# Level 1's loop on the parity form of the composite convolution, with folds one pair ahead and elementwise steps on GpSimd

## The reference: what is computed

```python
for i, typ in enumerate(('same', 'upsample', 'same', 'downsample')):
    s = style @ mod_w[i].T + mod_b[i]
    weight = SCALE * w[i] * s[:, None, :, None]
    weight = weight * rsqrt(sum(weight * weight) + EPS)
    out = conv(out, weight) + biases[i]      # with blur around types 2 and 4
```

```python
W = scales[:, 0][None, :] * q - zeros[:, 0][None, :]
out = einsum('bsi,io->bso', x, W) + bias
```

## Time and profile before

| | |
|---|---|
| median of 3 runs | 907.77 us (907.46 to 908.02) |
| profiled execution, its own time | 907.6 us |
| its span in the trace | 906.1 us |
| PE busy | 898.8 us, 99% of the span |
| DVE busy | 531.7 us, 59% |
| ACT busy | 459.8 us, 51% |
| POOL busy | 89.6 us, 10% |
| store of a pair by POOL, issue to landing (15 of them) | 3.0 us, median |
| granted TensorE clock | 1.000, the upper level (2.4 GHz), all through |

### The profile page before, as it was taken

How to read it: one execution, slowest core, us unless ns; L and a number is a source line. 1 busy time by engine, 2 the same in 40 slices (tenths; PEclk the granted TensorE clock), 3 DMA queues, 4 the chain that set the end, 5 groups by cost and what they waited for, 6 DMA issues and landing times.

```text
span 906.1 us, 15387 instructions
## 1 busy us (share of the span) xinstructions
PE 898.8 (99%) x5174; PEld 825.7 (91%) x5174; DVE 531.7 (59%) x1248; ACT 459.8 (51%) x881; POOL 89.6 (10%) x113
## 2 busy tenths in 40 slices
PE   9999999999999999999999999999999999999998
PEld 8889899899899899899899898888999999999998
DVE  8886445455455455365465465576755566665555
ACT  5955435435445455355355245477455656555540
POOL 0000000000000000000000020302111211111221
PEclk9999999999999999999999999999999999999999
DMA  8701101201201101101102112341222221222111
GB/s 293 247 3 69 69 23 46 69 23 46 69 16 53 50 25 64 46 23 69 46 23 69 62 53 70 65 167 44 93 84 81 93 69 69 69 93 83 57 71 70
DMA packets 33133, 64.30 MB, mean 71 GB/s; under 512 B 11728, under 2 KB 14032, under 8 KB 33104
## 3 DMA queue, kind: packets, MB, share of 16 engines
q1 hardware_dynamic: 24032, 30.90, 11.2%
q0 software_dynamic: 9072, 33.03, 9.7%
HBM read 47.14 MB, written 16.78 MB: 71 GB/s over the span
## 4 chain that ended last, share of the span: by engine, by line
PE 96%; DVE 2%; ACT 2%; issue 0%; ACTq 0%; DVEq 0%
PE conv_ps L184 8%; PE conv_ps L185 8%; PE conv_ps L186 8%; PE fold_ps L728 6%; PE prod_ps L1024 6%; PE prod_ps L1022 6%; PE prod_ps L1023 6%; PE prod_ps L989 5%; PE prod_ps L991 5%; PE prod_ps L990 5%; PE prod_ps L1098 4%; PE prod_ps L1097 4%; PE fold_ps L693 4%; PE turn_ps L943 3%; PE turn_ps L991 2%; PE turn_ps L990 2%
## 5 line engine op out<-in xcount | busy, mean ns | idle before, releaser
L1022 PE MATMUL prod_ps<-b_hi,xt 128*128 128x512 f32 x240 | 93.6, 390 | 0.0
L1024 PE MATMUL prod_ps<-b_hi,xt 128*128 128x512 f32 x240 | 93.5, 390 | 0.0
L1023 PE MATMUL prod_ps<-b_lo,xt 128*128 128x512 f32 x240 | 93.5, 389 | 0.0
L949 ACT ACTIVATE xt<-turn_ps 128x512 fp32r<-128x512 f32 x32 | 17.4, 594 | 136.9 <-PE turn_ps L943 136.9
L989 PE MATMUL prod_ps<-a_hi,xt 128*128 128x384 f32 x240 | 81.2, 338 | 0.0
L991 PE MATMUL prod_ps<-a_hi,xt 128*128 128x384 f32 x240 | 81.1, 338 | 0.0
L990 PE MATMUL prod_ps<-a_lo,xt 128*128 128x384 f32 x240 | 81.1, 338 | 0.0
L1097 PE MATMUL prod_ps<-quant,xt_hi 128*128 128x342 f32 x256 | 80.8, 320 | 0.0
L1098 PE MATMUL prod_ps<-quant,xt_lo 128*128 128x342 f32 x256 | 80.7, 320 | 0.0
L184 PE MATMUL conv_ps<-h_hi,e_hi 128*128 128x512 f32 (+1 forms) x204 | 75.5, 370 | 1.1 <-DVE h_lo L170 1.1
L1082 DVE SCALAR_TENSOR_TENSOR res<-prod_ps,norm,res 128x512 f32<-128x512 f32 x32 | 23.9, 751 | 87.8 <-PE prod_ps L1024 86.7
(11 more groups left out here) (313 smaller groups left out, 2404.0 us busy)
## 6 DMA issues: line engine op xcount, KB each, us to landing
x_in<-in_x SPq DMA_DIRECT2D x64, 128.0 KB, 2.7
res<-in_x POOLq DMA_DIRECT2D x16, 512.0 KB, 3.6
x_after_first<-res POOLq DMA_DIRECT2D x16, 512.0 KB, 2.9
x_in<-x_after_first SPq DMA_DIRECT2D x64, 128.0 KB, 2.7
res<-x_after_first POOLq DMA_DIRECT2D x16, 512.0 KB, 3.5
out_x<-res POOLq DMA_DIRECT2D x15, 512.0 KB, 3.0
a_raw<-in_adapter_in SPq DMA_DIRECT2D x8, 544.0 KB, 8.7
b_raw<-in_adapter_out SPq DMA_DIRECT2D x8, 512.0 KB, 6.9
```

What stands on the lines that cost most here:

```text
L1022: nc.tensor.matmul(prod_ps[n][:, :], bufs.xt_hi[:, k, :], bufs.b_hi[:, k, cols], start=(k == 0), stop=False)
L1023: nc.tensor.matmul(prod_ps[n][:, :], bufs.xt_hi[:, k, :], bufs.b_lo[:, k, cols], start=False, stop=False)
L1024: last = nc.tensor.matmul(prod_ps[n][:, :], bufs.xt_lo[:, k, :], bufs.b_hi[:, k, cols], start=False, stop=(k == KT - 1))
```

## The change

Four things, all in level 1's loop (the last is in code around it):

1. `pe_cond` becomes `pe_three`, with level 0's helpers for the data (`act_layer1_parity`, `act_parity_hi`, `dve_parity_lo`) and filters (`act_fold2_whole`, `act_filters`, `dve_filters`), and with `act_middle` and `dve_join` in the place of `act_cond`.
2. The folds run one pair ahead: step `i` applies the filters of `c` and makes those of `c + 1`.
3. The differences and the sums of filter tiles are made by POOL (`pool_differences`, `pool_filter_sums`), behind `load_residual` and ahead of the next `add_bias`.
4. `pe_turn` comes first in PE's step, and `dve_second_residual` is cut in two: parts 0 and 1 ahead of the split of `x`, part 2 between the two joins.

```diff
+        def pool_differences(pool, c, a, bufs):
+            data = bufs.data[a]
+            odd = data[:, ODD:ODD + SPAN]
+            pool.wait_ge(S.data_pads, DATA_PADS)
+            pool.wait_ge(S.layer1_scaled, 2 * c + a + 1)
+            nc.gpsimd.tensor_tensor(data[:, LEFT:LEFT + SPAN], data[:, EVEN:EVEN + SPAN], odd, ALU.subtract)
+            nc.gpsimd.tensor_tensor(data[:, RIGHT:RIGHT + SPAN], data[:, EVEN + 1:EVEN + 1 + SPAN], odd, ALU.subtract).then_inc(S.differences, 1)
+
+        def pool_filter_sums(pool, c, bufs):
+            pool.wait_ge(S.fold2_hi, 2 * c + 1)
...
+            nc.gpsimd.tensor_tensor(flat(whole[:, E_PAIRS:E_PAIRS + 2, :, :]), flat(whole[:, 0:E_PAIRS:2, :, :]), flat(whole[:, 1:E_PAIRS:2, :, :]),
+                                    ALU.add).then_inc(S.fold2_lo, 1)
...
+                c = f + 1 + AHEAD
+                for a in range(2):
+                    pool_differences(pool, c, a, buf1[slot])
+                if not isinstance(n, int) or j + 1 < SLOTS:
+                    pool_filter_sums(pool, c + 1, buf1[slot])
...
                 c = i + AHEAD
-                pe_layer1(pe, c, 0, bufs)
                 pe.wait_ge(S.x1_ready, evicted(i))
                 pe_turn(pe, i, bufs, True)
-                pe_layer1(pe, c, 1, bufs)
-                pe_fold3(pe, c, bufs)
-                pe_quant(pe, i, 0, bufs)
-                pe_fold2(pe, c, bufs)
-                pe_quant(pe, i, 1, bufs)
+                for a in range(2):
+                    pe_layer1(pe, c, a, bufs)
+                if left:
+                    pe.wait_ge(S.middle_scaled, 2 * c)
+                    pe_fold3(pe, c + 1, bufs)
+                for n in range(2):
+                    pe_quant(pe, i, n, bufs)
+                if left:
+                    pe_fold2(pe, c + 1, bufs)
                 pe_quant(pe, i, 2, bufs)
-                pe_cond(pe, c, 0, bufs)
+                pe_three(pe, c, 0, bufs, left > 0)
...
-                pe_cond(pe, c, 1, bufs)
+                pe_three(pe, c, 1, bufs, left > 0)
...
                 act_turn(act, i, bufs)
-                act_layer1(act, c, 0, bufs)
-                act_fold3(act, c, bufs)
-                act_layer1(act, c, 1, bufs)
-                act_fold2(act, c, bufs)
-                if not last:
+                act_filters(act, c, bufs)
+                act_layer1_parity(act, c, 0, bufs)
+                if left:
+                    act_fold3(act, c + 1, bufs)
+                act_layer1_parity(act, c, 1, bufs)
+                for a in range(2):
+                    act_parity_hi(act, c, a, bufs)
+                if left:
                     split(c + 1, bufs)
-                    act_fold_start(act, c + 1, bufs)
+                    act_fold2_whole(act, c + 1, bufs)
+                if left > 1:
+                    act_fold_start(act, c + 2, bufs)
+                act_middle(act, c, 0, bufs)
...
+                act_middle(act, c, 1, bufs)
                 for a in range(2):
-                    act_cond(act, c, a, bufs)
+                    act.wait_ge(S.cond_out, 2 * c + a + 1)
                     act_ends(act, c, a, bufs)
```

More of the change, by code:

```diff
@@ L867, in act_fold2_whole @@
             nc.scalar.activation(flat(whole[0:C, 0:E_PAIRS, :, C:P]), blocks[C:P, :, :], ACT.Identity)
[L868 to L869 removed]
+            last = nc.scalar.activation(flat(whole[C:P, 0:E_PAIRS - 1, :, C:P]), blocks[0:C, 2:2 * E_PAIRS, :], ACT.Identity)
+            if not bufs.first_sample:
+                last = nc.scalar.activation(whole[C:P, E_PAIRS - 1, :, C:P], bufs.e_hi[C:P, E_PAIRS - 1, :, C:P].bitcast(F32), ACT.Identity)
+            last.then_inc(S.fold2_hi, 1)
         def dve_filter_sums(v, c, bufs):
@@ L891, in dve_filters, with pe_three @@
             low(flat(bufs.sum_lo[:, :, :, :]), flat(bufs.whole[:, E_PAIRS:E_PAIRS + 2, :, :]), flat(bufs.sum_hi[:, :, :, :])).then_inc(S.fold2_ready, 1)
-        def pe_three(pe, c, a, bufs):
+        def pe_three(pe, c, a, bufs, ahead=False):
+            if a == 1 and ahead:
+                pe.wait_ge(S.fold2_hi, 2 * c + 3)
             if a == 0:
@@ L1120, in dve_second_residual @@
                     nc.vector.tensor_tensor(bufs.res[:, cols], bufs.res[:, cols], bufs.scaled[:, cols], ALU.add).then_inc(S.y_ready, 1)
-            if not last:
+            if not last and 2 in parts:
                 v.wait_ge(S.zeros_added, g + 1)
@@ L1189, in program @@
             b.xt_hi, b.xt_lo = T1(f"xt_hi1{n}", [P, KT, P], F32R), T1(f"xt_lo1{n}", [P, KT, P], F32R)
+        data1, whole1 = [T1(f"data1{a}", [P, DATA]) for a in range(2)], T1("whole1", [P, E_PAIRS + 2, 2, P])
+        for b in buf1:
+            b.data, b.whole = data1, whole1
+            b.sum_hi, b.sum_lo, b.right_hi, b.right_lo = buf0.sum_hi, buf0.sum_lo, buf0.right_hi, buf0.right_lo
         level1.close()
@@ L1355, in _, with second_step @@
             add_bias(FIRST % SLOTS, 1)
-            with pool.Fori(0, (END - FIRST - 1 - AHEAD) // SLOTS) as n:
-                for j in range(SLOTS):
[L1358 to L1363, removed]
+            def second_step(n, j):
+                f = SLOTS * n + (FIRST + j)
+                slot = (FIRST + j) % SLOTS
+                add_bias((slot + 1) % SLOTS, n + (1 if j + 1 < SLOTS else 2))
+                store_output(f, slot)
+                pool.wait_ge(S.y_stored, 16 * (f - NPAIR) + 16)
+                load_residual(f + SLOTS, slot)
+                c = f + 1 + AHEAD
[3 more added lines that the diff above has]
+                    pool_filter_sums(pool, c + 1, buf1[slot])
+            loops = (END - FIRST - 1 - AHEAD) // SLOTS
+            with pool.Fori(0, loops - 1) as n:
+                for j in range(SLOTS):
+                    second_step(n, j)
+            for j in range(SLOTS):
+                second_step(loops - 1, j)
             for f in range(END - 1 - AHEAD, END - 1):
@@ L1915, in _ @@
             dve_first_residual(v, f, buf0)
+            nc.vector.memset(whole1[C:P, E_PAIRS - 1, :, C:P], 0.0)
+            for a in range(2):
+                dve_data_pads(v, c, a, slot(c))
             edge_copies(v, set1, buf0)
```

89 lines of the change are left out of this document (56 added, 33 removed).

## The result

The changed kernel takes 917.19 us (median of 4 runs, 915.38 to 918.14); the kernel before took 907.88 beside it (907.46 to 908.02). The ratio is 1.010, interval 1.008 to 1.012: slower by 1.0%. The profiled execution took 916.77 us, with a span of 915.2, against 907.6 and 906.1 before. The granted clock is 1.000 in both of these executions, so nothing of their difference is the clock's.

The account below looks back on a forecast made before the run. PE was taken to bound the old kernel, a 17.7 us ring grown to 20.75 by collisions the new one. Twelve steps 244.35, + 3.6 at the start, - 238.0 before = +9.95 on 907.6: 917.5 us, range 903 to 922.

Parts of the forecast that it names:

- PE's saving, 1.22 us a pair: Level 1's convolutions on PE in parity form: 4.35 us a pair instead of 5.57, making a step 18.5 us.
- Start, +3.6: Ahead of the loop: +2.9 us for the fold that comes in on PE, +0.7 for the wait for the third `scaled`.
- The two collisions, +0.95 and +2.1: Split of `x` on VectorE: first half waits 0.95 us for GpSimd's sum of filters, second half 2.1 for `add_bias`.
- rival B: Sum of filters starts a little after VectorE's split of `x` instead of 0.15 before: 904 to 911 us, chance 0.20.
- the slack: Room of 0.8 us between the walk without collisions, 17.7, and PE's 18.5; the first step still has it.
- Rival C: Engines hardly hinder one another, so PE bounds eleven steps of 18.5 us: 895, range 892 to 898, chance 0.15.
- The differences: GpSimd's two differences of a=1, 257 columns: 0.74 us each, 1.6 for two with signals.
- The line: Cost estimate for GpSimd operations between measured sizes: 2.18 ns a column over 0.18 us.
- the ring: From a step's last join through ACT, POOL, ACT and DVE back to it: 17.7 us, 20.75 with collisions.
- the nine: The steps between the second and the last of level 1's loop: 20.75 us each, 186.75 together.
- The last step: Twelfth step, without fold: 16.5 us of PE work, plus waits of 0.8 for transposed data and 1.5 for `scaled`: 18.8.
- The one that waits gets the next turn: Between GpSimd and VectorE, a two-input SBUF operation waits for the other's whole operation, then goes next; shown waits 0.21, 0.45 us.

Follow-up runs that it names:

- experiment 4: Changed kernel with the loop's add_bias cut from 1024 columns to one, its place and semaphores kept: 896.55 us.
- Experiments 1 to 5: Changed kernel with differences and filter sums on VectorE 897.51 us; sums alone there 905.54; differences alone 911.52; add_bias cut to one column 896.55; in two halves 908.32.
- experiment 7: Changed kernel with add_bias moved from behind the sum of filters to ahead of the differences, directly behind load_residual: 919.29 us.
- experiment 6: Changed kernel with add_bias replaced at its place by a one-input GpSimd operation (res times 1.0, 128x1024): 902.84 us.
- experiment 1: Changed kernel with differences and sums of filters on VectorE, add_bias staying on GpSimd: 897.51 us.
- experiment 8: Kernel of experiment 7 with load_residual, the DMA issue ahead of add_bias, moved behind the sum of filters: 900.84 us.
- experiment 5: Changed kernel with add_bias as two GpSimd operations of 512 columns at its place: 908.32 us.
- experiment 9: Kernel of experiment 7 with a GpSimd wait between load_residual's DMA issue and add_bias, until sum_lo is done: 907.42 us.

## Why the prediction came out

- **PE's saving, 1.22 us a pair: right.** 4.32 us for a pair, first step 18.58 for 18.5, and 18.5 in every step of experiment 4.
- **Start, +3.6: right.** Between the first two sets of transposes lie 14.98 us; before it was 640.80 - 628.11 = 12.69, with a first convolution of 1.4 in it that now stands behind them. 14.98 - 11.3 = 3.7, of which 0.70 is the wait for `scaled` that was named.
- **The two collisions, +0.95 and +2.1: right**, to 0.1, and so were their order and the margin of it (`x_lo` comes up 0.14 behind the start of the sum; I had 0.15). It held in ten of the eleven steps that have a sum. In the first one the order was rival B's: the two `x_lo` begin at 656.34, the sum only at 656.67, the first `x_lo` goes free and the second takes 1.79; there the slack covered it, and PE did not wait for the transposes behind. Experiments 1 to 5 show that these collisions make the loss. Rival C is what the kernel is with nothing in the way: 895 foreseen, 896.55 and 897.51 measured.
- **The differences: mis-sized.** The line gave 0.74 us for 257 columns; they took 0.64. That takes 0.2 off the ring: second step 20.07 for 20.3, the nine 20.56 for 20.75. In all 1.9 us too much.
- **The last step: a wait missed.** From 866.58 to the first product behind it (887.07) are 20.49 us, where I had 18.8, so 1.7 too little. That step has no sum of filters, so `add_bias` follows the differences at once and meets `_lo` of a=0. At that place I had counted only a collision with a difference, and put it at nothing because VectorE waits there for ScalarE; `add_bias` I had left out of this step:

```profile
877.05 2.61 DVE L170 TENSOR_TENSOR right_lo<-data,right_hi 128x257 fp32r<-128x257 f32 x1
```

  PE stood 1.4 us for it. The two mistakes cancel: 244.2 us for the twelve steps, 244.35 foreseen. Where the trace ends within 0.7 us of the forecast, some of that is luck. The sum with these measured terms is still 0.8 above the 9.1 us between the two spans, and that lies in the kernel before: its steps are 19.80 us on average (640.80 to 858.59 is eleven of them), where the one that I read had 19.76, so its twelve steps take 238.55 us (from the first convolution at 639.39 to the first product behind them at 877.94), not 238.0; and it reaches its first transposes 0.23 later (628.11, now 627.88).
- **"The one that waits gets the next turn": right here, wrong as a rule.** It holds where the waiting one comes up during the other's operation, as all through the changed kernel, and fails behind a DMA issue (experiment 7). Had the change left `add_bias` there, the same working would have given 897 for a kernel of 919, and would have missed the falls of the clock too.

The Trainium skill, "SBUF — State Buffer", section "SBUF: two separate sides", says that whichever of the two engines starts first gets the shared port pair for the whole instruction. For operations with two inputs in SBUF on both sides the rows agree where one operation came up during the other: 2.14 us of waiting under one `add_bias` of 2.41. They do not agree where `sum_lo` came up during a DMA issue, 0.12 us before `add_bias` started (experiment 7): it came first and did not get its turn. For a GpSimd operation with one input, experiment 6 shows less than the whole: 0.8 us under one of 3.2.

## What to carry to other kernels

Before an elementwise operation is moved to GpSimd, list what VectorE runs beside it and read the operands of each: a two-input operation in SBUF that comes up during a two-input one of GpSimd waits until that one ends. Look at what stands behind the moved operation in GpSimd's queue as well, because it moves too; here the harm was done by an old operation that had been harmless where it was. If it must stand there, cut it into pieces, keep it off the engine's ring, or put the work on VectorE, where these differences take 0.42 us each and the sum 0.68; in experiment 1 `add_bias` still held VectorE in every step, and PE did not wait for it.

## What the runs showed of the hardware that was not expected

- A VectorE operation that comes up while GpSimd issues a DMA, with a ready two-input operation behind it, can be kept out of the whole run that follows: 5.56 to 5.68 us for an operation of 0.69, five times in one kernel. With `add_bias` alone behind the DMA, as in experiment 1, it lost to that one in five steps (3.16 to 3.20 us) and got in first in two (0.68). Without a ready operation behind the DMA issue it is not held at all (0.69). What in GpSimd's queue does this is not settled.

```profile
723.42 0.53 POOL L1368 DMA_DIRECT2D res<-x_after_first  x1 [3.06 <-DMA out_x<-res]
723.97 2.40 POOL L1373 TENSOR_TENSOR res<-res,bias 128x1024 f32<-128x1024 f32 x1
```

```profile
723.74 3.19 DVE L170 TENSOR_TENSOR sum_lo<-whole,sum_hi 128x512 fp32r<-128x512 f32 x1
```

- A GpSimd operation with one input slows a two-input VectorE operation from 0.75 to 1.52 us without holding it to the end.
- The granted clock can fall after a wait of PE of some 2 us. It fell after waits of 2.03, 2.07, 2.07 and 2.09 us (experiment 7), 2.29 (experiment 8) and 2.73 (experiment 5), for about 3.4 us each time. It did not fall after 1.99 in the changed kernel, nor after 2.71 in experiment 9, so what decides is open.
